# Gated cross-attention block: the order of three VectorE operations, and the end of the last batch rows

## The reference, cut to what matters

```python
# 16 heads of 16; attention from tokens to the 77 context rows
q, k, v = layernorm(x) @ Wq + bq, ctx @ Wk + bk, ctx @ Wv + bv
attn    = softmax(q k^T / 4);  o = attn v
x1      = x + tanh(g_xattn) * (relu(o @ W1 + b1) @ W2 + b2)
# 8 experts, two chosen for each token
n       = layernorm(x1)
p       = softmax(max(n @ gate_W + gate_b, 1e-4))
comb    = max(p, 0.1) of the two largest, divided by their sum
out     = x1 + tanh(g_ffn) / 2 * sum_e comb_e * (n @ expert_W[e] + expert_b[e])
```

## Time and profile before

| | us |
|---|---|
| three runs | 991.95, 992.25, 987.53 |
| median | 991.95 |
| the profiled execution, its own time | 988.13 |
| its span (first to last instruction) | 986.4 |

### The profile page before, as it was taken

How to read it: one execution, slowest core, us unless ns; L and a number is a source line. 1 busy time by engine, 2 the same in 40 slices (tenths; PEclk the granted TensorE clock), 3 DMA queues, 4 the chain that set the end, 5 groups by cost and what they waited for, 6 DMA issues and landing times.

```text
span 986.4 us, 26160 instructions
## 1 busy us (share of the span) xinstructions
PE 931.3 (94%) x9410; PEld 670.0 (68%) x9410; DVE 854.7 (87%) x2139; ACT 720.2 (73%) x1517; POOL 642.4 (65%) x792
## 2 busy tenths in 40 slices
PE   3679999999999999999999999999999999999987
PEld 2557777767776776776677677667767677777763
DVE  5787888988989888898898889889888988988875
ACT  4756878777787877777787777778777778777661
POOL 5445666667776567776666777666677766667743
PEclk8579999999999999999999999999999999999999
DMA  6000000000000000000000000000000000000000
GB/s 199 27 15 11 15 15 26 26 25 22 26 15 15 25 26 25 24 15 25 15 25 25 25 23 15 25 15 27 25 26 22 16 14 26 25 12 12 13 12 22
DMA packets 17471, 24.61 MB, mean 25 GB/s; under 512 B 2798, under 2 KB 8896, under 8 KB 17344
## 3 DMA queue, kind: packets, MB, share of 16 engines
q1 hardware_dynamic: 17344, 22.94, 7.4%
HBM read 14.54 MB, written 8.39 MB: 23 GB/s over the span
## 4 chain that ended last, share of the span: by engine, by line
PE 78%; DVE 10%; ACT 5%; issue 5%; POOL 1%; DMA 0%; POOLq 0%; ACTq 0%; DVEq 0%
PE e L740 28%; PE g L740 18%; PE t L923 9%; PE t L789 4%; PE g L940 3%; PE s L874 3%; PE s L811 2%; PE s L810 2%; PE s L809 2%; DVE row_max L1256 2%; PE g L749 2%; ACT p_f L557 2%; DVE acc L1211 2%; DVE p_lo L1194 2%; ACT p_hi L558 2%
## 5 line engine op out<-in xcount | busy, mean ns | idle before, releaser
L373 POOL TENSOR_TENSOR p_lo<-p_f,p_hi 77x512 f16<-77x512 f32 x160 | 184.4, 1168 | 221.5 <-ACT p_hi L558 221.5
L740 PE MATMUL e<-we_hi,x2T_lo 128*128 128x512 f16 x496 | 188.5, 380 | 4.8 <-DVE acc L1211 4.6
L740 PE MATMUL e<-we_hi,x2T_hi 128*128 128x512 f16 x496 | 187.8, 379 | 0.0
L740 PE MATMUL e<-we_lo,x2T_hi 128*128 128x512 f16 x496 | 187.8, 379 | 0.0
L557 ACT ACTIVATE p_f<-t 77x512 f32<-77x512 f32 x256 | 152.6, 596 | 27.5 <-PE t L789 25.0
L1211 DVE SCALAR_TENSOR_TENSOR acc<-e,comb,acc 128x256 f32<-128x256 f32 x307 | 146.2, 476 | 13.8 <-PE e L740 11.5
L558 ACT ACTIVATE p_hi<-t 77x512 f16<-77x512 f32 x256 | 152.6, 596 | 0.0
L1256 DVE TENSOR_REDUCE row_max<-s 128x6 f32<-128x462 f32 (+1 forms) x192 | 108.6, 579 | 19.8 <-PE s L874 19.2
L809 PE MATMUL s<-v_hi,p_lo 77*128 77x17 f16 x1024 | 98.3, 172 | 9.1 <-DVE p_lo L1194 6.1
L809 PEld LDWEIGHTS s<-v_hi,p_lo 77*128 77x128 f16 x1024 | 84.0, 96 | 29.5 <-issue 10.6
L636 ACT ACTIVATE scaled<-e,comb 128x256 f32<-128x256 f32 x126 | 56.4, 475 | 65.2 <-PE e L740 65.2
(11 more groups left out here) (194 smaller groups left out, 2881.0 us busy)
## 6 DMA issues: line engine op xcount, KB each, us to landing
x_sb<-in_x SPq DMA_DIRECT2D x32, 256.0 KB, 2.6
out<-acc SPq DMA_DIRECT2D x32, 256.0 KB, 2.0
we_f<-in_L_ffn_expert_W SPq DMA_DIRECT2D x2, 1024.0 KB, 9.5
y_sb<-in_ctx SPq DMA_DIRECT2D x32, 57.8 KB
w_f<-in_L_xattn_W SPq DMA_DIRECT2D x2, 512.0 KB, 7.4
wq_f<-in_L_xattn_Wq SPq DMA_DIRECT2D x1, 256.0 KB, 4.1
wkv_f<-in_L_xattn_Wk SPq DMA_DIRECT2D x1, 192.0 KB, 2.9
wkv_f<-in_L_xattn_Wv SPq DMA_DIRECT2D x1, 192.0 KB, 3.9
```

Of the source, the lines that this page charges most:

```text
L373: pool.tensor_tensor(p_lo[:, r].rearrange("m h n -> m (h n)"), p_f[:, r, :], p_hi[:, r].rearrange("m h n -> m (h n)"), ALU.subtract).then_ ...
L740: mm = pe.matmul(out_ap, a, c, start=(first and i == 0), stop=(last and i == n - 1))
```

## The change

VectorE: in the middle of a step `add_expert(7, 1)` stands ahead of `take_max(b, 0)`, and at its beginning `yT_low` ahead of `p_low(m, 0)`. In the last two steps: product 5 of row 30 stands ahead of the gate's scores of row 31, the combination's transposes follow product 1 and the bias product follows product 2. For the last row the sum of `acc` and the biases is made by VectorE, one half of the tokens after product 6 and the other after product 7, and SP stores each half by itself.

```diff
@@ sync: store
             def store(pair, u, b):
-                sp.wait_ge(acc_done, b + 1)
-                sp.dma_start(out_pairs[pair, u], acc[:, u]).then_inc(stored[u], 16)
+                if b < B - 1:
+                    sp.wait_ge(acc_done, b + 1)
+                    sp.dma_start(out_pairs[pair, u], acc[:, u]).then_inc(stored[u], 16)
+                    return
+                for t in range(T):
+                    sp.wait_ge(acc_done, b + 1 + t)
+                    sp.dma_start(out_pairs[pair, u][:, t], acc[:, u, t]).then_inc(stored[u], 16)
...
-            for u in range(2):
-                sp.wait_ge(stored[u], 16 * (B // 2))
+            sp.wait_ge(stored[0], 16 * (B // 2))
+            sp.wait_ge(stored[1], 16 * (B // 2 + T - 1))
@@ gpsimd: step
                 if has(s, -3):
                     add_scaled(f, fu)
+                if has(s, -3) and f < B - 1:
                     add_biases(f, fu)
@@ tensor: step
-                if s == B + 1:
-                    gate_scores(e, eu)
                 if last and s <= B + 1:
                     experts(f, fu, 5, s - 3, (lambda: transposes_y(pair, b, u)) if front else None)
                 elif front:
                     transposes_y(pair, b, u)
-                if first and s <= B:
+                if first:
                     gate_scores(e, eu)
...
                 if s == B + 1:
                     experts(e, eu, 1, s - 2)
+                    combT_transposes(e, eu)
                     experts(e, eu, 2, s - 2)
+                    expert_biases(e)
                     experts(e, eu, 3, s - 2)
-                    combT_transposes(e, eu)
                     experts(e, eu, 4, s - 2)
-                    expert_biases(e)
                     experts(e, eu, 5, s - 2)
@@ vector: a new function
+            def add_last_biases(b, u, t):
+                dve.wait_ge(scaled_added, 2 * b + 2)
+                dve.wait_ge(expert_added, 2 * len(ADDED) * (b + 1) - 2 * (T - 1 - t))
+                dve.tensor_tensor(acc[:, u, t], acc[:, u, t], bias_sum[:, u, t], ALU.add).then_inc(acc_done, 1)
@@ vector: step
                 if front:
                     xnT_low(b)
+                if front:
+                    yT_low(b)
                 if mid:
                     p_low(m, 0)
-                if front:
-                    yT_low(b)
...
                 if last:
                     add_expert(f_pair, f, fu, 6, 1, s - 3)
+                if last and f == B - 1:
+                    add_last_biases(f, fu, 0)
...
                 if last:
                     add_expert(f_pair, f, fu, 7, 0, s - 3)
-                if front:
-                    take_max(b, 0)
                 if last:
                     add_expert(f_pair, f, fu, 7, 1, s - 3)
+                if last and f == B - 1:
+                    add_last_biases(f, fu, 1)
+                if front:
+                    take_max(b, 0)
```

More of the change, by code:

```diff
@@ L1445, in step @@
                     add_expert(f_pair, f, fu, 7, 0, s - 3)
+                if last:
+                    add_expert(f_pair, f, fu, 7, 1, s - 3)
+                if last and f == B - 1:
+                    add_last_biases(f, fu, 1)
                 if front:
                     take_max(b, 0)
-                if last:
-                    add_expert(f_pair, f, fu, 7, 1, s - 3)
                 if mid:
```

## The result

The changed kernel takes **1027.13 us** (median of 4 runs, 1025.68 to 1027.82), the kernel before 989.87 in as many runs (987.53 to 992.25): a ratio of **1.0371 [1.0347, 1.0396]**, slower by 37.3 us where 12.3 us less were forecast. The profiled execution took 1027.82 us, 1.7 of them beside its span of 1026.1.

The account below looks back on a forecast made before the run. TensorE, busy 94% of the span, was taken as the bound, with two waits on VectorE; 10.2 + 0 + 1.31 + 0.81 = 12.3 us off the median 991.95 gave 979.6 us, range 966.2 to 990.1.

Parts of the forecast that it names:

- the 0.2 us is absorbed there: VectorE's gate after the reordered pair: `gshift`, held until GpSimd's `p_lo` ends anyway, hides VectorE's 0.2 us delay.
- The rule that the prediction quoted: Shared port: a two-SBUF-input VectorE instruction and a GpSimd instruction reading SBUF exclude each other; the second to start waits.
- The bound without that cover: If `gshift` hid nothing, VectorE runs 0.2 us later until the normalisation ends, leaving 0.14 of the 0.34 us gain.
- move together: Argument against `comb` losing the port: VectorE and GpSimd are both tied to the same exponentials.
- rival three: VectorE's `comb` loses the port to GpSimd in all 29 steps: 49.0 us more, 1028.6 us; chance 0.14.
- The step of 30 us: Sign of a wrong forecast: steps of 30 us, with `comb` at 1.17 us in most steps.
- the 1.69 us: Extra time of the profiled step where `comb` was held, from down projections 59.23 us apart over two steps.
- The gain of `yT_lo` first: Key/value product starts 0.34 us sooner per step, bounds 0.16 and 0.42; 10.2 us over 30 steps.
- The swap of `acc`: Last accumulation ahead of the first maximum, mid-step: counted as nothing, bounds nothing and 9.6 us.
- the new wait for `h_lo` that was named: Down projection: TensorE arrives 0.33 us sooner after the `acc` swap and waits 0.33 us there for `h_lo`.
- 1.31 + 0.81 = 2.1 us: Last steps: 1.31 us from an expert product filling TensorE's idle time, 0.81 net from splitting the last sum.
- the cover that was forecast: At the end, GpSimd's second sum of scaled products finishes 1.4 us ahead of VectorE's first last sum.

Follow-up runs that it names:

- the table above: Six kernels compared behind `gs`: listing of the last `p_lo`, end of `khT`, step; from 7.86, 7.90, 28.77 us (before) to 7.43, 7.31, 30.12 us (changed).
- the end alone: Kernel before with only the edits of the last two steps: 987.83 us, ratio 0.9976 [0.9965, 0.9988].
- the kernels with the key block's wait: Changed kernel, GpSimd's first key block waiting for VectorE's last `p_lo`: 981.74 us; with the gate's exponential also behind the fourth group of attention exponentials: 975.40 us.
- the 360 steps: Thirty steps each of twelve kernels without that wait: `p_lo` listed ahead of `khT`'s end in 256, always first; 0.09 to 0.12 us behind in 81, always lost.

## Why the prediction was wrong

**The step that failed** is "the 0.2 us is absorbed there". VectorE did leave the pair about 0.2 us later, as stated. But the cover was looked for at `gshift`, which ended with GpSimd's `p_lo` in the earlier trace rows; `gs`, two places ahead of it in the queue, had a margin of 0.10 us to that `p_lo`'s start, and was not costed. Held, it pushes `gshift` to 562.20, 0.45 us behind the `p_lo`'s end (561.75) instead of beside it. The rule that the prediction quoted speaks of instructions with two SBUF inputs; `gs` has one, `graw`, and was held all the same.

**The bound without that cover was too mild.** "VectorE would run 0.2 us later up to the end of the normalisation" took VectorE and GpSimd as the only ones to move. `gshift` reaches ScalarE through `gexp`, GpSimd through `p_f`, and VectorE again through GpSimd's low parts, while `khT` stays at its place. So the engines do not "move together", the ground on which rival three got only 0.14.

**Rival three had the kind and the price right, the place wrong.** 1028.6 us was worked out for `comb` losing in each step; 1027.13 came. In the repeating step `comb` lost nothing; the last `p_lo` lost 1.23 us and the last `h_lo` 1.01, in TensorE's waits 1.0 and 0.9. The step of 30 us was what the prediction would have read as its own error, but not with `comb` at 0.23 us. The size agrees for two reasons: any such loss is about one GpSimd instruction of 1.2 us, and the step that the 1.69 us were read from holds the second meeting too. There, behind the held `comb`, `xb` is listed at 325.07 us and the last `h_lo` at 325.31, and `h_lo` takes 1.33 us. That the total came within 1.5 us is chance, as two losses less two removed waits make it up.

**What held.** The gain of `yT_lo` first: 0.34 us per step forecast, 0.40 where nothing gives it back (28.77 to 28.37), near the upper bound of 0.42. The swap of `acc`: nothing forecast, nothing measured, with the new wait for `h_lo` that was named (10.4 us in 27 waits of the weight loads). The section weighed there, "Who interferes with whom" in "SBUF — State Buffer" of the Trainium skill, says more than the prediction used: it names `tensor_scalar` among the operations that can take both ports and meet GpSimd when their operands allow it, and says that the order of issue, not the shape, decides who is held. `gs`, a `tensor_scalar` on 16 numbers, agrees with both (0.18 us ahead of GpSimd's `p_lo`, 1.12 behind it). The last `p_lo` does not follow the order of the listed starts: in the changed kernel it is listed 0.16 us ahead of the key block (568.10, 568.26) and is held for it. There the order of the inputs decides, as in the table above.

**The end.** Forecast 1.31 + 0.81 = 2.1 us; the end alone gave 2.4. In the changed kernel, rows of PE, DVE and POOL, and the page's DMA issues (KB each, us to landing):

```profile
1007.83 0.38 PE L746 MATMUL s<-we_hi,x2T_hi 128*128 128x512 f16 x1
1008.33 0.18 PE L746 MATMUL g<-gw_hi,x2T_lo 128*128 128x8 f16 x1
...
1007.58 0.69 DVE L1325 TENSOR_TENSOR x2T_lo<-g,x2T_hi 128x512 f16<-128x512 f32 x1 [0.25 <-ACT x2T_hi L633]
...
1022.08 0.42 DVE L1222 TENSOR_TENSOR acc<-acc,bias_sum 128x256 f32<-128x256 f32 x1
...
1023.52 0.42 DVE L1222 TENSOR_TENSOR acc<-acc,bias_sum 128x256 f32<-128x256 f32 x1
...
1019.41 1.27 POOL L412 TENSOR_TENSOR bias_sum<-bias_sum,scaled 128x512 f32<-128x512 f32 x1
...
out<-acc SPq DMA_DIRECT2D x2, 128.0 KB, 1.7
```

The product fills the idle time of the earlier trace rows and the gate's scores still follow `x2T_lo` (1007.58 + 0.69 = 1008.27, scores at 1008.33). GpSimd is done at 1020.68, 1.4 us ahead of the first last sum, the cover that was forecast; a last sum takes 0.42 us (0.43 taken). From the gate's scores to the end of the span it was 986.4 - 966.33 = 20.07 us, and is 1026.1 - 1008.33 = 17.77: 2.3 less. The store of 128 KB landed in 1.7 us against 2.0 for 256 KB, a gain of 0.3 that the sum had at zero. The estimate by the Trainium skill, "DMA: Bandwidth & Descriptors", section "Anatomy of one DMA", for DMAs that GpSimd issues, was 0.3 too. By the same estimate the two sizes would take 2.6 and 2.3 us; SyncE's stores here took 2.0 and 1.7, and the measurement decides.

**What stays open.** Why the instruction that is ready first wins was not tried by itself: in each kernel of the table GpSimd was still busy with a `p_lo` at that moment. The table and the 360 steps show the rule for this one pair of instructions, not its mechanism. That the kernels with the key block's wait reach their second `gs` some 3 us sooner was not followed up either.

## What to carry to other kernels

Where two engines share a port, a reorder is costed by margins, not by durations: list, for each pair of neighbours on the two engines, who is ready first and by how much, and follow a shift of 0.2 us through every queue that reads the shifted value, across engines, until it comes back. A gain on one engine can remove the slack that hid another engine's wait; here an independent exponential that stood in the queue ahead of its turn was the link, and moving it one place (one group of exponentials) made a loss of 3.7% a gain of 1.6%. A wait added on the engine that should come second is a cheap first test.

## What the hardware showed unexpectedly

- An instruction of 16 numbers per partition, with one input in SBUF, took 1.12 us instead of 0.18 because it started 0.08 us behind a GpSimd instruction instead of 0.10 ahead.
- Between VectorE's `p_lo` and GpSimd's next instruction, margins of 0.04 to 0.19 us decide, while GpSimd is still at the one before: ready 0.12 us too late, VectorE waited for a second GpSimd instruction and took 1.97 us instead of 0.74.
- One copy of 0.41 us more per step on ScalarE made a kernel 50 us faster, and one wait more on GpSimd 45.
